# Attentive GRU stage: attention keys and query of four batches summed in PSUM, the candidate's input share added there too

## The reference, cut to what matters

```python
def step(h, x_t):
    hid = jnp.broadcast_to(h[:, None, :], (Bn, Sn, Hn))
    combined = jnp.concatenate([hid, enc_hiddens], axis=2)
    score = jnp.tanh(jnp.einsum('bsk,kh->bsh', combined, W_att))
    score = jnp.einsum('bsh,h->bs', score, V_att[:, 0])
    attn = jax.nn.softmax(score, axis=-1)
    context = jnp.einsum('bs,bsh->bh', attn, enc_hiddens)
    inp = jnp.concatenate([x_t, context], axis=1)
    gz, gr, gh = jnp.split(inp @ Wi + b, 3, axis=1)
    rz, rr, rh = jnp.split(h @ Uh, 3, axis=1)
    z = jax.nn.sigmoid(gz + rz)
    r = jax.nn.sigmoid(gr + rr)
    hh = jnp.tanh(gh + r * rh)
    h_new = z * h + (1.0 - z) * hh
    return (h_new, h_new)
_, outs = jax.lax.scan(step, last_hidden, jnp.swapaxes(dec_seq, 0, 1))
```

## Time and profile before

| | us |
|---|---|
| median of 3 runs | 5760.1 |
| the runs | 5753.4, 5760.1, 5780.1 |
| profiled execution, its own time | 5762.9 |
| span of the profiled execution | 5761.1 |
| first to last `part` (L1302) of the recurrent stage | 1781.3 |
| TensorE busy over the span | 4907.7 (85%) |
| VectorE busy | 2920.8 (51%) |
| ScalarE busy | 2109.4 (37%) |
| GpSimd busy | 585.3 (10%) |

### The profile page before, as it was taken

One profiled execution on the slowest core, in us unless ns is written; L12 is line 12 of the kernel. 1 busy time (PEld: TensorE's weight loads), 2 busy tenths in 40 slices (PEclk: granted clock), 3 DMA queues, 4 the chain that ended last, 5 costly groups with the idle time before them and its releaser, 6 DMA issues. The chain is left out here.

```text
span 5761.1 us, 115322 instructions
## 1 busy us (share of the span) xinstructions
PE 4907.7 (85%) x46515; PEld 3114.7 (54%) x46515; DVE 2920.8 (51%) x9818; ACT 2109.4 (37%) x4155; POOL 585.3 (10%) x1312
## 2 busy tenths in 40 slices
PE   4389999999999996588989888898869897788784
PEld 3256666666666664355545555455534574555563
DVE  5634444444444443477666777677636323334343
ACT  2223222222222221166656666566534332122221
POOL 3300000000000002211111111111110000000000
PEclk7689899898998997699999999999979798898896
DMA  0010000000000001100000000000000001000000
GB/s 24 7 32 2 2 2 2 2 2 2 2 2 2 2 2 50 54 6 4 9 4 9 4 5 5 7 8 4 6 38 1 1 1 41 1 1 1 1 1 9
DMA packets 33174, 51.08 MB, mean 9 GB/s; under 512 B 8596, under 2 KB 24118, under 8 KB 32000
## 3 DMA queue, kind: packets, MB, share of 16 engines
q1 hardware_dynamic: 29312, 39.67, 2.1%
q10 hardware_dynamic: 2304, 2.11, 0.1%
q0 software_dynamic: 1024, 1.78, 0.1%
HBM read 39.03 MB, written 4.19 MB: 8 GB/s over the span
## 5 line engine op out<-in xcount | busy, mean ns | idle before, releaser
L1157 PE MATMUL psum<-g_still,ident_bf 128*128 128x512 bf16 (+6 forms) x3388 | 1018.9, 359 | 19.1 <-issue 17.5
L2277 DVE TENSOR_REDUCE l_m<-psum 128x2 bf16<-128x512 f32 x768 | 503.8, 693 | 164.8 <-PE psum L1881 161.7
L1157 PEld LDWEIGHTS psum<-g_still,ident_bf 128*128 128x128 bf16 x3388 | 409.1, 139 | 144.1 <-issue 84.6
L2153 ACT ACTIVATE l_probs<-psum,l_mcol 128x1024 f32<-128x1024 f32 x384 | 406.7, 1110 | 175.5 <-PE psum L1919 175.5
L1881 PE MATMUL psum<-l_kb,l_qmb 32*128 32x256 bf16 x1536 | 299.0, 276 | 70.6 <-DVE l_m L2277 52.0
L1237 ACT ACTIVATE g_th<-g_pre 128x256 f32<-128x256 f32 x512 | 192.2, 418 | 348.8 <-DVE g_pre L1270 348.8
L1919 PE MATMUL psum<-l_qm,l_keys 32*128 32x256 f32 x3072 | 268.3, 422 | 14.6 <-issue 14.6
L1270 DVE TENSOR_TENSOR g_pre<-g_encp,psum 128x256 f32<-128x256 f32 x512 | 192.9, 418 | 168.4 <-PE psum L1188 120.9
L2164 ACT COPY l_heads_out<-psum 128x256 f32<-128x256 f32 (+1 forms) x292 | 130.3, 446 | 367.6 <-PE psum L1945 184.8
L1945 PE MATMUL psum<-l_probs,l_v 128*32 128x256 f32 x3072 | 222.5, 410 | 46.2 <-DVE l_o L2317 28.7
L2277 DVE TENSOR_REDUCE l_cm<-psum 128x4 bf16<-128x256 f32 x400 | 166.3, 428 | 178.2 <-PE psum L1881 178.0
(11 more groups left out here) (571 smaller groups left out, 10138.6 us busy)
## 6 DMA issues: line engine op xcount, KB each, us to landing
s_w<-in_S_w SPq DMA_DIRECT2D x16, 256.0 KB, 5.0
f_w<-in_F_w SPq DMA_DIRECT2D x2, 2048.0 KB, 12.3
l_wf<-in_L_W SPq DMA_DIRECT2D x7, 576.0 KB, 3.7
l_w<-in_L_W SPq DMA_DIRECT2D x1, 3072.0 KB, 10.4
l_wc<-in_L_W SPq DMA_DIRECT2D x7, 384.0 KB, 2.9
l_nw<-in_L_nw SPq DMA_DIRECT2D x1, 2304.0 KB, 7.9
l_wa<-in_L_W SPq DMA_DIRECT2D x7, 320.0 KB, 2.7
h_w<-in_H_W ACTq DMA_DIRECT2D x16, 129.0 KB, 3.0
```

The source lines that it names most:

```text
L1157: pe.matmul(psum[:, bank, 0:cols], cst["ident_bf"][:], still[:, 0:cols], start=True, stop=True)
L2153: act.activation(probs[:, u % 2, chunk, :].rearrange("p (g n) -> p g n", g=GROUP), psum[:, 0:GROUP, S * chunk:S * chunk + S], ACT.Exp, bia ...
L2277: dve.tensor_reduce(place, psum[:, c.bank(("max", u, g)), 0:x.tiles * x.width] .rearrange("p (t k) -> p t k", t=x.tiles), AX.X, ALU.min)\
```

## The change

Scores' inputs are no longer summed by VectorE for both halves.

- First half (even batches): the keys are multiplied anew in every step (`key_part`, 256 columns, the keys' weights times the context columns), and the query products run over 256 columns, the 4 batch columns repeated 64 times each (`every_key`), into the same PSUM bank. ScalarE reads the sum there.
- Second half: one product of 4 columns with the summed state `h` into bank 7, one add on VectorE to `encp1`.
- The candidate's token share goes into bank 6 as a product with the identity (`input_part(2, 6, s)`), ahead of the context share, and VectorE's add `gh` is gone.
- The three state products move behind the scores; the candidate's goes to bank 2 and is copied to SBUF (`rh`) before the transposition uses that bank.
- Fillers: 18 to 16 at the head of a pass; in a step 4,864 columns become 1,024 (left: 192 between the scores, and 192, 512 and 128 at the gates).

```diff
-                    keep_busy(3, 512, 18)
+                    keep_busy(3, 512, 16)
+                    key_part()
                     input_part(1, 5, 0)
                     input_part(0, 4, 0)
...
                             pe.wait_ge(sig["kept_part_ready"], s)
-                            pe.matmul(psum[:, 0, 0:B], wa_half[:], zh[:], start=True, stop=False)
-                            keep_busy(3, 256)
+                            query_part(wa_half[:], zh[:], stop=False)
                             pe.wait_ge(sig["new_part_ready"], s)
-                            pe.matmul(psum[:, 0, 0:B], wa[:, 0, :], part[:], start=False, stop=True)\
-                                .then_inc(sig["query_ready"], 1)
-                            keep_busy(3, 256)
+                            query_part(wa[:, 0, :], part[:]).then_inc(sig["first_pre_ready"], 1)
                             pe.wait_ge(sig["state_ready"], s)
-                        pe.matmul(psum[:, 7, 0:B], uh[:, 2, :], hs, start=True, stop=True)\
-                          .then_inc(sig["state_products_ready"], 1)
-                        pe.matmul(psum[:, 5, 0:B], uh[:, 1, :], hs, start=False, stop=False)
-                        pe.matmul(psum[:, 4, 0:B], uh[:, 0, :], hs, start=False, stop=False)
-                        keep_busy(3, 448, 2)
+                        pe.matmul(psum[:, 7, 0:PAIRS], wa[:, 0, :], half(hs, 1), start=True, stop=True)\
+                          .then_inc(sig["query_ready"], 1)
+                        if s >= 1:
+                            pe.wait_ge(sig["candidate_input_ready"], s)
+                        input_part(2, 6, s)
...
                             if i == 0:
-                                keep_busy(3, 320)
+                                keep_busy(3, 192)
                         last.then_inc(sig["scores_ready"], 1)
-                        keep_busy(3, 512, 3)
-
+
+                        pe.matmul(psum[:, 2, 0:B], uh[:, 2, :], hs, start=True, stop=True)\
+                          .then_inc(sig["state_product_ready"], 1)
+                        pe.matmul(psum[:, 5, 0:B], uh[:, 1, :], hs, start=False, stop=False)
+                        pe.matmul(psum[:, 4, 0:B], uh[:, 0, :], hs, start=False, stop=False)
+
+                        pe.wait_ge(sig["state_product_taken"], s + 1)
                         pe.wait_ge(sig["exp_ready"], s + 1)
...
-                        keep_busy(3, 384, 2)
+                        if s + 1 < STEPS_A_PASS:
+                            key_part()
                         pe.wait_ge(sig["attnT_ready"], s + 1)
```

On VectorE and ScalarE:

```diff
-                        for i in range(2):
-                            act.wait_ge(sig["tanh_input_ready"], 2 * s + i + 1)
-                            act.activation(th[:, i, :, :], pre[:, i, :, :], ACT.Tanh).then_inc(sig["tanh_ready"], 1)
+                        act.wait_ge(sig["first_pre_ready"], s + 1)
+                        act.activation(th[:, 0, :, :], psum[:, 0, 0:HB].rearrange("p (b s) -> p b s", b=PAIRS), ACT.Tanh)\
+                           .then_inc(sig["tanh_ready"], 1)
+                        act.wait_ge(sig["second_pre_ready"], s + 1)
+                        act.activation(th[:, 1, :, :], pre1[:], ACT.Tanh).then_inc(sig["tanh_ready"], 1)
...
                         dve.wait_ge(sig["query_ready"], s + 1)
-                        query = psum[:, 0, 0:B].rearrange("p (b i) -> p i b", i=2)
-                        for i in range(2):
-                            dve.tensor_tensor(pre[:, i, :, :], encp[:, i, :, :],
-                                              query[:, i, :].unsqueeze(2).to_broadcast([P, PAIRS, C]), ALU.add)\
-                                .then_inc(sig["tanh_input_ready"], 1)
+                        dve.tensor_tensor(pre1[:], encp1[:], psum[:, 7, 0:PAIRS].unsqueeze(2).to_broadcast([P, PAIRS, C]), ALU.add)\
+                           .then_inc(sig["second_pre_ready"], 1)
...
+                        dve.wait_ge(sig["state_product_ready"], s + 1)
+                        dve.tensor_copy(rh[:], psum[:, 2, 0:B]).then_inc(sig["state_product_taken"], 1)
...
-                        dve.wait_ge(sig["context_h_turned"], s + 1)
-                        dve.tensor_tensor(gh[:], psum[:, 6, 0:B], gx(2, s), ALU.add).then_inc(sig["candidate_part_ready"], 1)
+                        dve.wait_ge(sig["gate_h_ready"], s + 1)
                         dve.wait_ge(sig["reset_ready"], s + 1)
-                        dve.wait_ge(sig["candidate_part_ready"], s + 1)
-                        dve.scalar_tensor_tensor(u2[:], u[:], 0.5, gh[:], ALU.mult, ALU.add)\
+                        dve.scalar_tensor_tensor(u2[:], u[:], 0.5, psum[:, 6, 0:B], ALU.mult, ALU.add)\
```

More of the change, by code:

```diff
@@ L1045, in attentive_gru @@
         wa_half = sb("wa_half", [P, D])
-        gh, kept, tr, tz, u, u2, cand, omz, zh, part = (sb(n, [P, B]) for n in ("gh", "kept", "tr", "tz", "u", "u2", "cand", "omz", "zh", "part"))
+        rh, kept, tr, tz, u, u2, cand, omz, zh, part = (sb(n, [P, B]) for n in ("rh", "kept", "tr", "tz", "u", "u2", "cand", "omz", "zh", "part"))
         still = sb("still", [P, 512], BF16)
@@ L1070, in _ @@
                               start=True, stop=True).then_inc(sig["encw_ready"], 1)
+                pe.matmul(psum[:, 0, 0:PAIRS * C], wa[:, 1, :], ctxT[:].rearrange("p (b i s) -> p i b s", i=2, s=C)[:, 1, :, :],
+                          start=True, stop=True).then_inc(sig["encp_ready"], 1)
                 pe.wait_ge(sig["encp_taken"], 1)
@@ L1106, in _ @@
                 act.wait_ge(sig["encp_ready"], 1)
[L1107 removed]
+                act.copy(encp1[:].rearrange("p b s -> p (b s)"), psum[:, 0, 0:PAIRS * C]).then_inc(sig["encp_taken"], 1)
                 for p in range(PAIRS):
@@ L1157, in keep_busy, with input_part @@
                             pe.matmul(psum[:, bank, 0:cols], cst["ident_bf"][:], still[:, 0:cols], start=True, stop=True)
+                    def input_part(gate, bank, s):
+                        pe.matmul(psum[:, bank, 0:B], cst["ident"][:], gx(gate, s), start=True, stop=False)
+                    def key_part():
+                        pe.matmul(psum[:, 0, 0:HB], wa[:, 1, :], keys[:, 0, :, :], start=True, stop=False)
+                    def query_part(w, rows, stop=True):
+                        return pe.matmul(psum[:, 0, 0:HB], w, every_key(rows), start=False, stop=stop)
                     def context_part(gate, bank, ready):
@@ L1165, in context_part, with turn_part @@
                         last.then_inc(sig[ready], 1)
[L1167 to L1171, removed]
+                    def turn_part(i, bank, ready):
+                        pe.matmul(psum[:, bank, 0:B], crows[:, i, :], shares[:], start=False, stop=True)\
                           .then_inc(sig[ready], 1)
-                    keep_busy(3, 512, 18)
+                    keep_busy(3, 512, 16)
+                    key_part()
                     input_part(1, 5, 0)
@@ L1219, in _ @@
                         pe.wait_ge(sig["context_h_taken"], s + 1)
-                        turn_part(1, 6, "context_h_turned", start=True)
+                        turn_part(1, 6, "gate_h_ready")
                         keep_busy(3, 192)
```

14 lines of the change are left out of this document (7 added, 7 removed).

## The result

The changed kernel takes **6607.6 us** (median of 4 runs, 6593.7 to 6609.0), the kernel before in the same runs 5759.7 us: **slower, ratio 1.145 [1.142, 1.149]**, +848 us. Its profiled execution has a span of 6591.9 us.

The account below looks back on a forecast made before the run. Bound: a closed chain over all engines, 6.33 us a step at full clock, plus 0.5 for the clock. 256 x (10.2 - 6.85) = +858 us on 5762.9 is 6621, the median 3 lower: 6618 us; range 5640 to 6720.

Parts of the forecast that it names:

- main case: Recurrent stage: clock falls early in each pass, stays low until the next; 6618 us, case range 6350 to 6720, chance 0.50.
- What bounds: a closed chain and the clock: Each recurrent step is a chain over all engines, 6.33 us at full clock; the clock adds 0.5 us on the mean.
- A second place of the fall: Query products to key product, over 2.5 us with one 192-column filler left, becomes a second place where the clock falls.
- It stays low: After some five full-clock steps a pass, the clock stays low until the next pass's 16 fillers; clock near 0.55.
- Full-clock step 6.39: Sum of the changed step's parts at full clock: 6.33 + 0.06 = 6.39 us, bounds 6.25 and 6.5.
- rival D: Products with repeated columns stream at half rate: +230 us, 5990; chance 0.20 shared with another rival.
- The state products' move costs nothing: Six narrow passes behind the scores fit beside minimum and exp; transposition at 3.10 us, no cost, no slack left.
- Candidate: gain lost: Without the add, `part` gains 0.06 us, but the product with `zh` hangs on the z gate and gains nothing.
- Keys: Key product after the transposition puts the context products at 3.94 us against 3.88: 0.06 lost a step.
- Low step 10.5: Step at 1.2 GHz, summed by pieces on 6.39: 4.3 us more, less 0.2 off waits, taken as 10.5 us.
- the 0.41 of the earlier trace: Steps of the kernel before lengthen 0.41 us for each us at low clock; this gave a 10.8 us low step.
- Rival A: Wide products do the fillers' work, clock stays full, faster: -118 us, 5642 (5700 with occasional falls); chance 0.22.

Follow-up runs that it names:

- Run 1: Kernel before with only the change's filler cut (4,864 to 1,024 columns a step): 6181.7 us, ratio 1.071.
- run 4: Kernel before with wider fillers at the gates (192 and 128 to 320) and behind both query products (256 to 448): 5621.8 us, ratio 0.975.
- run 10: Kernel of run 4 with the three state products behind the scores, three 512-column fillers ahead of them, two 448s gone: 5593.0 us, ratio 0.974.
- run 6: Kernel of run 4 with repeated columns, key product and one add instead of two; state products stay ahead of the scores: 5691.4 us, ratio 0.988.
- run 5: Kernel of run 4 with the candidate's token share on TensorE, add `gh` gone, two 448-column fillers cut to 384: 5748.0 us, ratio 0.999.
- run 2: Changed kernel with fillers added: 256 columns ahead of first scores, 512 instead of 192 between scores: 5942.4, 5934.3, 5664.4 and 5955.9 us.
- runs 2 and 8: The 8 here: kernel of run 2 with 40 instead of 16 opening fillers in each pass: 6248.7, 5968.2, 5679.4 and 6237.9 us.
- run 9: Kernel of run 2 with the gate fillers of run 4 (192 and 128 become 320): 5954.2, 5680.2, 5955.6 and 5948.8 us.
- run 3: Changed kernel with one burst of 16 fillers of 512 columns at the 33rd step of each pass: 6605.7 us, ratio 1.145.

## Why the prediction was right

6618 us were predicted for 6607.6 measured, on the main case. The mechanism held; that the number is met within 11 us is luck in part. The low step was set 0.1 us too long (some 24 us in all) and 256 steps were counted where 252 intervals lie inside the passes (14 us); against that, the steps at full clock were set too many (some 38 us), and the three nearly cancel. The range, 5640 to 6720, took in both signs, so a time inside it says little. Point by point:

- *What bounds: a closed chain and the clock.* Right. Run 1 loses 409 us and run 4 gains 150 by fillers alone, with the computation untouched.
- *A second place of the fall.* Right. All 92 low stretches in the stage of before begin near `part`; those inside passes start 0.9 to 2.1 us after it, behind the gates. After the change there is one in each of passes 2 to 4, and each begins 3.2 to 3.4 us after `part`, at the transposition: behind the stretch from which the fillers had gone. The one in the first pass is at the transposition too, in the first step. The fall at 1138.40, in windows (fillers alone, L1167; their busy time, clock behind it):

```profile
1135.00:1138.40 3.40, 0.31 (x2) 0.10 (x1) 1.00 0.02 7
1138.40:1141.80 3.40, 0.00 (x0) 0.00 (x0) 0.50 0.00 0
```

  Against the earlier trace rows: 0.31 us of fillers ahead of the fall instead of 1.35, and none instead of 2.55 in the low stretch. The two query products in the first of these windows (1.11 us of PE) did not hold the clock, nor did 1.22 us of key product in the second bring it back; in the first of them TensorE is recorded busy for 3.17 of 3.40 us. The two steps before ran the same instructions at 1.00 throughout, so this is where the clock can fall, not where it must.
- *It stays low.* Right, and more so than I said: 638.3 us at 0.50 in one piece, then much the same in passes 3 and 4; but for the last pass it ended with the 16 fillers at the head of the next. I had a clock of 0.55 and five steps at full clock in each pass; it was 0.50 to 0.52, with two or three such steps and a mixed one, in the first pass none.
- *Full-clock step 6.39.* Measured 6.49, inside the bounds. In the first step of a pass, where the product with `zh` starts 0.10 before `part` as the sum had it (0.09): first tanh predicted 1.06, measured 1.05; add of the second half 1.18, 1.17; second scores 2.09, 2.09; transposition 3.10, 3.19; context products 3.94, 4.04. The query products end at 1.01 and repeated columns stream at the full rate: rival D is out, since at half rate the tanh would start near 1.9. Counted from one product with `zh` to the next this step takes 6.49 us as the later ones do, and nearly the whole 0.10 lies in one place. The step "cost nothing, with no slack left" for the state products is where 0.09 was missed: the transposition starts 0.14 us after the end of the exp (1125.38), in run 10 0.06 (1337.48). In both the exp ends 0.96 us after the start of the second scores and the third state product starts 0.72 after it, so neither makes the difference. Run 10 has no copy `rh` and one wait fewer there; that this is the reason is argued, not shown. (A small misreading in the sum: in the earlier trace rows the second scores start 0.37 us after their tanh ends, not 0.3.)
- *The state products' move costs nothing.* Wrong in a way that the sum hid. I credited 0.13 us of earlier scores to the fillers gone from ahead of them; run 10 has more filler columns there and gets 0.14 from moving the narrow products away, and run 6, without the two 448s but with the state products still in place, gets nothing (2.26 against 2.23). The move is the good part of the change.
- *Candidate: gain lost.* Right on the reason (the product with `zh` hangs on TensorE, not on `part`): in the change `part` starts 0.03 us ahead of that product where it was 0.09 behind it, and the product itself gains nothing. On the kernel of run 4 the price is another: run 5 gives +0.16 us, not 0.
- *Keys.* Right: from the transposition to the context products 0.84 us were predicted, and it is 0.85 in the change and in run 6, 0.65 before. The 0.06 of the sum is this 0.20 less the 0.13 of earlier scores; run 6 has the one without the other, hence its +0.23. The three runs' prices do not add up: 6.33 - 0.14 + 0.23 + 0.16 = 6.58 against 6.49 measured. Since the transposition accounts for the excess of the change, the candidate's product costs it nothing, perhaps because it finds room once the state products are gone (argued).
- *Low step 10.5.* Measured 10.40: 3.91 us over 6.49 where the pieces gave 4.1 over 6.39. By the 0.41 of the earlier trace rows it would be 6.49 / 0.59 = 11.0. That ratio came from steps whose fillers stretch as well, and the changed kernel has few (argued; run 2, with more of them, has 10.89).

Rival A is refuted for the changed kernel as it stands, but run 2 shows that it was near: with 576 filler columns a step more, whole passes run at 1.00, with a clock that falls in others. The Trainium skill (TensorE: Matmul & The Clock Gate, "Why this matters for your kernels") would have this kernel at full clock, as it has no idle gap of microseconds. The runs here do not agree: in the first pass of run 2 TensorE is recorded busy for 685.10 of 685.46 us, and the granted clock is 0.50 from end to end.

## What to carry to other kernels

Before wide work is taken off TensorE in a latency-bound loop, look where its clock falls now, and ask for each stretch of the new order whether it resembles the stretch ahead of such a fall; a busy share of 98%, which the stage had before (1745.40 of 1781.28 us), says nothing about that. Price each part of a change on a version whose clock is steady: here, each alone on the kernel of run 4, one part gained 0.14 us a step and two lost 0.23 and 0.16, and under the moving clock none of it could be seen. Do not take such prices for a sum. A narrow product with slack belongs behind the work that others wait for, not ahead of it.

## What the runs showed of the hardware

- One program, one loop, two steady levels: a pass is 6.49 us a step at 2.4 GHz or 10.89 at 1.2 GHz, from its first `part` to its last (runs 2 and 8; 6.52 or 11.00 in run 9). In these runs the lower one ended only at the opening fillers of the next pass. What made a pass low was a fall at the transposition of its first step.
- After a burst that restored the clock (run 3) it was lost again within three steps.
- Tanh of 128 x 256 takes 384 ns when it reads PSUM (L1255 of the changed kernel) and 416 when it reads SBUF (L1258); I had kept 0.42.
- A float32 product over 256 repeated columns costs what one over 256 stored columns does: 0.70 us for L1173 with stored, 0.68 for L1176 with repeated columns, both with two passes, in the same step.
